# Attention and feed-forward over 16 batches on one core: x2T in two PSUM banks, the blocks' sum in two halves, three moved pieces of work

## What is computed

```
x = x + xattn(layernorm(x), ctx, ctx)
  scores = einsum(qg, kg) * scale            # per pair of blocks, 64 x 64
  attn = softmax(scores)                     # over the block's 64 keys
  out = segment_sum(attn @ vg, rows) @ Wo.T
x = x + ffn(layernorm(x))
  shared  = relu(xf @ sw1 + sb1) @ sw2 + sb2          # hidden size 1024
  routing = expert top1(token): relu(xf @ w1[e] + b1[e]) @ w2[e] + b2[e]
```

## Time and profile before

| | us |
|---|---|
| runs (median of 3) | 946.83 (944.99 to 947.7) |
| the profiled execution's own time | 948.77 |
| its span in the profile | 946.6 |
| PE busy | 807.7 (85%) |
| DVE busy | 598.4 (63%) |
| ACT busy | 493.3 (52%) |
| POOL busy | 420.3 (44%) |

### The profile page before, as it was taken

How to read it: one execution, slowest core, us unless ns; L and a number is a source line. 1 busy time by engine, 2 the same in 40 slices (tenths; PEclk the granted TensorE clock), 3 DMA queues, 4 the chain that set the end, 5 groups by cost and what they waited for, 6 DMA issues and landing times.

```text
span 946.6 us, 23198 instructions
## 1 busy us (share of the span) xinstructions
PE 807.7 (85%) x7862; PEld 670.6 (71%) x7862; DVE 598.4 (63%) x1226; ACT 493.3 (52%) x1108; POOL 420.3 (44%) x773
## 2 busy tenths in 40 slices
PE   3277877899998999898999989898989899988984
PEld 3146656586877868685968778686869596868884
DVE  3767584676758575776767575757577676646331
ACT  2373444436465555546464646455564646465542
POOL 3644324334344453635445544445363554455401
PEclk8587998979999999999999999999999999999998
DMA  8657232244435244344454453534434444414720
GB/s 269 172 150 252 78 102 67 76 137 142 151 110 185 88 147 149 107 148 136 135 153 144 128 172 95 172 110 133 152 115 137 152 133 137 142 46 134 253 83 23
DMA packets 97386, 128.17 MB, mean 135 GB/s; under 512 B 14655, under 2 KB 82623, under 8 KB 97088
## 3 DMA queue, kind: packets, MB, share of 16 engines
q1 hardware_dynamic: 89760, 107.89, 37.3%
q0 software_dynamic: 6624, 18.95, 5.9%
q10 hardware_dynamic: 960, 0.79, 0.4%
HBM read 90.80 MB, written 37.04 MB: 135 GB/s over the span
## 4 chain that ended last, share of the span: by engine, by line
PE 58%; DVE 15%; DMA 12%; ACT 6%; SPq 3%; issue 3%; POOL 1%; ACTq 1%; POOLq 0%; DVEq 0%
PE hid L502 19%; PE acc L671 13%; PE nd L596 10%; DVE T L1144 5%; DMA QP<-scratch_m 5%; PE work L580 4%; DMA scratch_m<-mT 3%; PE work L624 3%; PE work L502 2%; PE work L555 2%; DVE nmax L1125 2%; PE work L610 2%; DVE T L1141 2%; ACT h L925 1%; DVE Xs L1078 1%
## 5 line engine op out<-in xcount | busy, mean ns | idle before, releaser
L1404 POOL TENSOR_TENSOR hl<-h,hh 128x256 fp32r<-128x256 f32 x228 | 169.0, 744 | 351.2 <-ACT hh L925 351.1
L908 ACT ACTIVATE PT<-work 128x512 f32<-128x512 f32 x256 | 139.3, 600 | 58.4 <-PE work L580 55.8
L1144 DVE RECIPROCAL T<-nd 128x256 f32<-128x256 f32 x64 | 112.1, 1752 | 77.8 <-PE nd L596 74.0
L925 ACT ACTIVATE h<-hid,bias 128x256 f32<-128x256 f32 x144 | 69.0, 480 | 117.1 <-PE hid L502 117.1
L502 PE MATMUL hid<-Xs,W 128*128 128x256 f32 x816 | 115.1, 296 | 10.8 <-DVE Xs L1078 10.8
L502 PEld LDWEIGHTS hid<-Xs,W 128*128 128x128 f32 x816 | 105.1, 199 | 17.7 <-issue 10.8
L671 PE MATMUL acc<-w_hi,hh 128*128 128x256 f32 (+1 forms) x528 | 110.7, 292 | 0.0
L671 PE MATMUL acc<-w_lo,hh 128*128 128x256 f32 (+1 forms) x528 | 105.4, 281 | 0.0
L502 PE MATMUL hid<-Xr,W 128*128 128x256 f32 x768 | 105.3, 287 | 0.0
L596 PE MATMUL nd<-PT,V 128*32 128x256 f32 x1024 | 83.3, 398 | 25.4 <-DVE T L1146 22.5
L1125 DVE TENSOR_REDUCE nmax<-work 128x8 f32<-128x512 f32 x128 | 82.3, 685 | 35.1 <-PE work L555 35.0
(11 more groups left out here) (184 smaller groups left out, 1511.5 us busy)
## 6 DMA issues: line engine op xcount, KB each, us to landing
W<-w1q SPq DMA_DIRECT2D x64, 512.0 KB, 5.6
KP<-scratch_k SPq DMA_DIRECT2D x192, 64.0 KB, 2.3
QP<-scratch_q SPq DMA_DIRECT2D x180, 64.0 KB
scratch_k<-T SPq DMA_DIRECT2D x16, 512.0 KB, 3.5
scratch_q<-T SPq DMA_DIRECT2D x16, 512.0 KB, 3.3
yt<-yq SPq DMA_DIRECT2D x17, 260.0 KB, 2.8
xt<-xq SPq DMA_DIRECT2D x17, 256.0 KB, 3.8
xin<-x SPq DMA_DIRECT2D x16, 256.0 KB, 3.8
```

What stands on the lines that cost most here:

```text
L908: nc.scalar.activation(PT[:, j % 4].rearrange("p t q -> p (t q)"), work[:, BANK[("st", j)], :], ACT.Exp).then_inc(sem["exp_done"], 1)
L925: last = nc.scalar.activation(dst, hid[:, u % 2, a, :], ACT.Relu, bias=bias[:, 2 * u + a:2 * u + a + 1])
L1144: nc.vector.reciprocal(T[:, p, :], nd[:, p % 2, 1, :]).then_inc(sem["inverted"], 1)
L1404: nc.gpsimd.tensor_tensor(R(hl[:, u % 2, a]), h32[:, u % 2, a], hh[:, u % 2, a], ALU.subtract).then_inc(sem["hl_done"], 1)
```

## The change

Seven edits, all in the order of work or in where it is put:

1. `prep_tokens` puts the first chunk of x2T in the first half of its `work` bank and the second chunk in `hid[:, 1, 0]`; each chunk has its own high and low part on ACT and DVE (128x256 each in place of 128x512), and `shared_up(n, 0)` waits for the second chunk only halfway through its first product.
2. `attention_out` runs in two halves: the first waits for pairs 0 to 3 of T, the second for all eight. 32 matmuls of 64 columns in place of 16 of 2x64.
3. On PE each `shared_down` stands one place later: 0 behind visit 2, 1 behind visit 3, 2 behind the tile's transposes, 3 behind the q projection. ACT's `shared_relu(n, 3)` moves behind the split of mT, DVE's `finish_shared` behind q's low part.
4. The guessed pairs of iterations 3 to 15 are 2, 5, 7 in place of 2, 3, 6, 7.
5. Batch 1's x and context are loaded ahead of batch 0's bounces through DRAM, and its norm stands ahead of batch 0's maxima on DVE (before, in their middle); POOL's part of it stands ahead of the weights' splits.
6. ACT splits the first four weight pieces ahead of issuing its 12 spreads of q, not behind.
7. Behind the loop, the last batch's tile transposes stand behind `shared_up(3)` and `shared_down(2)`, and SP loads two registers ahead of the weights, not behind.

```diff
-GUESSED_EARLY, GUESSED = (1, 3, 5, 7), (2, 3, 6, 7)
+GUESSED_EARLY, GUESSED = (1, 3, 5, 7), (2, 5, 7)
-    "x2T": ("x2_lo", 1), "xr": ("xr_lo", 1), "rk": ("ranked", 1),
+    "x2T": ("x2_lo", DC), "xr": ("xr_lo", 1), "rk": ("ranked", 1),
+        def x2T_chunk(c):
+
+            return work[:, BANK["x2T", 0], 0:SEQ] if c == 0 else hid[:, 1, 0, :]
...
                 for n, (s, m) in enumerate(steps):
+                    if second and n == len(steps) // 2:
+                        pe.wait_ge(*second)
...
-                pe.wait_ge(sem["t_done"], PAIRS * (i + 1))
-                pairs = T[:, :, :].rearrange("p (c q) t -> p q c t", c=DC)
-                for r in range(NBLK):
-                    queries = slice(BLOCK * r, BLOCK * r + BLOCK)
-                    for q in range(4):
-                        mm = nc.tensor.matmul(bank[32 * q:32 * q + 32, :, queries], hsum[:, r, :],
-                                              pairs[:, q, :, queries], start=True, stop=True)
+                for c in range(DC):
+                    pe.wait_ge(sem["t_done"], PAIRS * i + 4 * c + 4)
+                    for r in range(NBLK):
+                        queries = slice(BLOCK * r, BLOCK * r + BLOCK)
+                        for q in range(4):
+                            mm = nc.tensor.matmul(bank[32 * q:32 * q + 32, c, queries], hsum[:, r, :],
+                                                  T[:, 4 * c + q, queries], start=True, stop=True)
...
                 pe.wait_ge(sem["ln2_done"], i + 1)
-                transposes(bank, xhat2, "x2T_full")
+                if type(i) is not int or i > 0:
+                    pe.wait_ge(sem["relu_done"], 2 * last_odd(i) + 2)
+                transposes(bank, xhat2, "x2T_full", apart=hid[:, 1, 0, :])
...
-                    shared_down(n, 0)
                 visit(i, 2, more)
                 if shared:
+                    shared_down(n, 0)
                     shared_up(n, 2)
+                visit(i, 3, more)
+                if shared:
                     shared_down(n, 1)
-                visit(i, 3, more)
...
```

More of the change, by code:

```diff
@@ L250, in guess_count @@
         def guess_count(i, p):
-            return len(GUESSED) * i + guessed(i).index(p) + 1
+            done = guessed(i).index(p) + 1
+            if type(i) is int and i < 3:
+                return len(GUESSED_EARLY) * i + done
+            return len(GUESSED) * i + 3 * (len(GUESSED_EARLY) - len(GUESSED)) + done
         def inverses(i, p):
-            return (PAIRS - len(GUESSED)) * i + p + 1 - sum(q <= p for q in guessed(i))
+            done = p + 1 - sum(q <= p for q in guessed(i))
+            if type(i) is int and i < 3:
+                return (PAIRS - len(GUESSED_EARLY)) * i + done
+            return (PAIRS - len(GUESSED)) * i + done - 3 * (len(GUESSED_EARLY) - len(GUESSED))
         def shared_unit(n, u):
@@ L460, in _ @@
                     .then_inc(sem["padded"], 16)
+            rows = [sp.value_load(left[0:1, e:e + 1], min_val=0, max_val=QROWS - TILE) for e in range(2)]
             for u in range(UNITS):
@@ L501, in split_product, with transposes @@
                 for n, (s, m) in enumerate(steps):
+                    if second and n == len(steps) // 2:
+                        pe.wait_ge(*second)
                     mm = nc.tensor.matmul(dst, R(s), R(m), start=n == 0, stop=n == len(steps) - 1)
                 return mm
-            def transposes(bank, src, done):
+            def transposes(bank, src, done, apart=None):
                 for c in range(DC):
                     for t in range(TT):
-                        mm = nc.tensor.transpose(bank[:, SEQ * c + P * t:SEQ * c + P * t + P],
-                                                 src[:, t, P * c:P * c + P], id32[:, :])
-                mm.then_inc(sem[done], 1)
+                        to = bank[:, SEQ * c + P * t:SEQ * c + P * t + P]
+                        if apart is not None and c > 0:
+                            to = apart[:, P * t:P * t + P]
+                        mm = nc.tensor.transpose(to, src[:, t, P * c:P * c + P], id32[:, :])
+                    if apart is not None or c == DC - 1:
+                        mm.then_inc(sem[done], 1)
             def front_xT(n, bank=None):
@@ L646, in ranks, with up @@
                                  skip_group_check=True).then_inc(sem["rk_full"], 1)
-            def up(g, u, weights, tokens):
+            def up(g, u, weights, tokens, second=None):
                 if type(g) is not int or g >= 2:
@@ L654, in up @@
                                        [(weights[:, u, 0, c, cols], weights[:, u, 1, c, cols]) for c in range(DC)],
-                                       [(tokens[:, 0, c, :], tokens[:, 1, c, :]) for c in range(DC)])
+                                       [(tokens[:, 0, c, :], tokens[:, 1, c, :]) for c in range(DC)],
+                                       second if a == 0 else None)
                 mm.then_inc(sem["hid_full"], 1)
@@ L767, in iteration @@
                 if tile:
+                    shared_down(n, 3)
                     tile_up(m, 0)
@@ L842, in _ @@
             shared_down(last, 1)
-            tile_tokens(last, work[:, 0, :])
             shared_up(last, 3)
             shared_down(last, 2)
+            tile_tokens(last, work[:, 0, :])
+            shared_down(last, 3)
             tile_up(last, 0)
-            shared_down(last, 3)
             tile_up(last, 1)
@@ L940, in tokens_high @@
             def tokens_high(i):
-                high(i, "x2T_full", work_bank("x2T"), Xs[:, 0], "x2_hi")
+                for c in range(DC):
+                    high(DC * i + c, "x2T_full", x2T_chunk(c), Xs[:, 0, c], "x2_hi")
             def table_relu(e):
@@ L967, in iteration @@
                     splits(i, u + 1)
-                    if tile or shared and u < UNITS - 1:
+                    if shared and u < UNITS - 1:
                         shared_relu(n, u)
@@ L1037, in _ @@
             projection_high(3)
+            for n in range(EARLY_PIECES):
+                split_high(n)
             act.wait_ge(sem["first_q_bounced"], 16)
@@ L1043, in _ @@
             front_v(0, acc[:, :, :])
-            for n in range(EARLY_PIECES):
-                split_high(n)
             iteration(0, False, False, True)
@@ L1056, in _ @@
             tile_relu(last - 1, 3)
-            for u in range(UNITS - 1):
+            for u in range(UNITS):
                 shared_relu(last, u)
             tile_high(last, work[:, 0, :].rearrange("p (c t) -> p c t", c=2))
-            shared_relu(last, UNITS - 1)
             tile_relu(last, 0)
@@ L1191, in shared_low @@
             def shared_low(i):
-                low(i, "x2_hi", work_bank("x2T"), Xs[:, 0], Xs[:, 1], "x2_lo")
+                for c in range(DC):
+                    low(DC * i + c, "x2_hi", x2T_chunk(c), Xs[:, 0, c], Xs[:, 1, c], "x2_lo")
             def tile_low(n, src, tokens=Xr):
@@ L1341, in _ @@
                     split_low(n)
+            norm1_apply(1)
             for j in range(4):
```

39 lines of the change are left out of this document (21 added, 18 removed).

## The result

The changed kernel takes 935.5 us (median of 5 runs, 933.55 to 941.65), the kernel before 944.99 (5 runs in the same series, 943.21 to 947.7). The ratio is 0.990, 95% interval 0.987 to 0.993: 9.5 us faster, a measured gain of 1%. The forecast was 930.0 with a range of 919 to 942. The profiled execution of the changed kernel is the slowest of its five (941.65, of which 939.5 are the span); the one of before took 948.77. So the two profiles differ by 7.1 only, and where the time went is read from stretches that are alike, not from the ends.

A forecast was written before the change was run, and what follows sets the result against it. PE's matmuls and the short waits between them were taken as the bound. Terms -7.2 (loop), -6, -1.3, -2.8, -1.9, -1.0 and +1.7 (clock) sum to -18.5 from 948.77; it took 930, range 919 to 942.

The forecast's parts named there:

- One sign that the prediction had named for being wrong: In the profile after: a clock of 0.5 to 0.8 in many iterations would show the forecast wrong.
- 0.7 for x2T: Loop iteration, PE's wait before the first shared_up: two banks gain 0.7 us, at least 0.3, at most 0.76.
- pairs and halves: Loop iteration's second part: new guessed pairs and attention_out in halves end it 1.2 us earlier (0.4 to 1.7).
- The rival in which halves cost as much as the whole: attention_out: each half costs 1.0 us, 0.35 less gained in each of 12 iterations, 934; chance 0.1.
- The late downs: Loop iteration, visit 2: shared_down one place later gives PE a new wait of 1.6 us for DVE's maxima (1.2 to 1.9).
- the first part: Loop iteration from x2T to the first values: ends 0.6 us later (0 to 1.2), ACT's relus and exps bounding its end.
- one more fall: Granted clock in the loop: the new waits at visit 2 lower it once more, +1.7 us (0 to +7).
- slower, by a fall in each iteration: Loop: the new wait lowers the clock in each iteration, 1.7 us for each of 13, 950; chance 0.06.
- The start: DVE's chain to batch 0's last maxima: stats, wait for rstd and xhat go out of it, -6 us (-3 to -8).
- the rival in which the start gains little, because the spreads are late: Start: spreads late in the full DMA queues, so little is gained there, 934; chance 0.1.
- Batch 0's end, iterations 1 and 2: Half sum and split x2T win 1.3 us at batch 0's end; earlier visits win 2.8 in iterations 1 and 2.
- Iteration 15 and behind the loop: Iteration 15: -1.9 us, its new wait being shorter; behind the loop, shorter waits for tokens and a transfer: -1.0.

The follow-up runs named there:

- e1: The changed kernel with all shared_down and their relu and sum put back to their old places, the rest of the change kept: 918.7 us.
- e8: e1 with the guessed pairs 2, 3, 6, 7 again in place of 2, 5, 7: 929.36 us.
- e7: e1 with attention_out in one piece again, behind all eight pairs: 920.25 us.
- e3: The changed kernel with shared_down(0) alone put back ahead of the second visit: 922.85 us.
- e5: The changed kernel with x2T's two chunks in one bank again, split in one pass on each engine: 936.3 us.
- e2: The kernel before with only the shared_down, their relu and sum moved one place later: 956.85 us.
- e10: e1 with the loads of x and context of batch 1 placed behind the two bounces: 919.16 us.
- e12: e1 with the edits of e9 and e10 together: 917.96 us.
- e6: e1 with the start undone: batch 1's loads, norm and deviation and ACT's early splits in their old places: 920.74 us.
- e4: The changed kernel with its edits behind the loop undone: 936.03 us.
- e11: e1 with the edits behind the loop undone: 917.44 us.
- e9: e1 with the bias issued ahead of three weight units and the next tile's tokens ahead of W1's last two units: 919.54 us.

## Why the prediction was right, and where it was off

**Sign, size, mechanism.** Faster was right, and 935.5 lies in the forecast's own 923 to 936, at its upper end. It is 5.5 above the point forecast. The gain is 9.5 where 16.8 were forecast; 1.8 of what is missing comes of the kernel before, which ran at 945.0 here and not at 946.8. Profile against profile the forecast was further off: -7.1 for -18.5, as the profiled execution of the changed kernel is 6.1 above its median. So that the median lies inside the range owes something to luck. By the stretches above, the clock, the start and the part behind the loop are what was put too well, and a period without a fall gained more than forecast. One sign that the prediction had named for being wrong came in part: a clock near 0.57 in five iterations of 12.

**x2T, pairs, halves.** Predicted 0.7 for x2T. In the old order (e1) all three together give 51.5 - 49.55 = 1.95, of which pairs are 0.8 and halves 0.4 (e8, e7), and 0.75 is left for x2T, which was not undone alone in that order. Predicted for pairs and halves was 1.2; measured 0.8 + 0.4. These steps hold within 0.1. The second half costs 0.58, where I took 0.65 with 0.5 as the lower bound. The rival in which halves cost as much as the whole is out.

That half is 32 instructions of 64 columns in 0.58 us, 18 ns each. The Trainium skill, TensorE: Matmul & The Clock Gate, section Back-to-back issue gap, gives an issue floor of some 25 ns for each, and by that page it would be 0.8 us, an estimate. The trace does not agree: it has 0.58, with four column groups in turn.

**The late downs.** I had put this move at a cost of 1.3 an iteration (the first part 0.6 later in spite of x2T's 0.7), and an iteration at 50.8. Measured 1.1 (e1 against the changed kernel) and 50.65; 0.85 gained where I had 0.6 to 0.65. So the prediction knew that one part of the change ate more than half of what the others give, and the wait at visit 2 stands where it was forecast: 0.54 and 0.69 for 0.7 and 0.9. The wait of 0.41 to 0.47 for the shifted rows was not worth removing in this way: it is back in e1, which is the faster kernel. One step was wrong in its reason: I said that the end of the first part is then set by ACT's relus and exps. There is a wait for ACT, but only of 0.35; e3 shows that the waits at visit 2 are most of the 1.1.

**The clock: the mis-sized term.** I had one more fall, +1.7. There were four more in the 12 periods, and what they took is 5 x 1.6 less the 0.6 of before, 7.4; with 12 x 0.85 = 10.2 gained, that makes the -2.8 of the table. e1, e3 and e5 take the waits away or shorten the first, and the falls are gone. I had argued that two waits of 1.6 together, behind the pairs, lowered the clock once in 12, and that new ones of the same size would do so once. That was wrong, and the sum of the waits alone does not decide it. Behind the pairs, 0.47 and 1.13, 2.2 us apart, gave one fall in 12 in the kernel before and in e2, and two in e8. At visit 2, 0.54 and 0.69, 1.2 us apart, gave five, though their sum is smaller; 0.2 and 0.69 gave none in e2 and none in e5. The rival "slower, by a fall in each iteration" had the mechanism and its price right; with five of 12 it took back most of what the iterations won, and not the sign.

The Trainium skill, TensorE: Matmul & The Clock Gate, section A second HAM failure mode: psum-queue depth-cycling, describes a kernel whose PE pauses briefly and often around its PSUM banks and whose clock goes back and forth between the two levels; the rows of this kernel agree, with waits of 0.5 and 0.7 us for banks that DVE still reads and a granted clock of 0.57 behind them.

**The start.** Predicted -6, and the two profiles differ by 4.1 at the first maxima. DVE's stats, norm and wait went out of its chain as forecast: PE's wait for the last maxima is 2.19, where it was 6.98. PE's timeline shows what came in their place (the earlier trace rows is the last of them before):

```profile
28.48 0.79 PE L570 MATMUL work<-KP,QP 48*128 48x256 f32 x4 [10.70 <-DMA QP<-scratch_q]
34.10 0.79 PE L570 MATMUL work<-KP,QP 48*128 48x256 f32 x4 [4.40 <-DMA QP<-scratch_q]
...
43.42 0.47 PE L585 MATMUL work<-id,nmax 128*128 128x128 f32 x1 [2.19 <-DVE nmax L1154]
```

The first score came 1.9 later, and the second visit waits 4.40 for its spread, where it waited 3.01 for DVE before. I had let the delay of the spreads and the gain of ACT's early splits cancel; the delay won. That is the rival in which the start gains little, because the spreads are late; that full queues are the reason is not shown, since e10 and e12 issued the spreads earlier and the first score came no sooner. e6 against e1 leaves 0 to 2 us for the whole start in time, so -6 was too much by 4 or more.

**Batch 0's end, iterations 1 and 2.** Predicted -4.1, the profiles say -5.0; the waits before batch 1's and 2's transposed maxima fell from 2.43 each to 0.85 and 0.69, 3.3 together for the 2.8 forecast. The waits were right; what they are worth is not shown. e1 has the old order and both waits of 2.43 again, and its stretch is 157.2, shorter than the changed kernel's 159.9.

**Iteration 15 and behind the loop.** Predicted -2.9, the profiles say +4.8. For the edits behind the loop the times say nothing that can be told: e4 is 0.5 above the changed kernel and e11 1.3 below e1. What I missed is in SP's queue: with the order moved, the relus of the tile come to wait for a bias that had been early enough before, as it stands behind three weight units. I had looked at PE's waits and named relu, low part and sum as the next bound, but not the 4 KB in front of the relu.

## What to carry to other kernels

Work that is moved out of one wait leaves the place where it stood: ask first what it was covering there. Here one `shared_down` hid the DVE maxima of the visit ahead. Moving it cost 0.7 us of the 1.1 that the late order costs in an iteration, and the falls of the clock. Judge each part of a change in the order in which it will stand: the split of x2T is worth 0.75 a period in one order, and in the other 0.35 less what it does to the clock. Issuing one transfer ahead of others can move the wait to the next: in e9 PE's waits behind the loop went from 4.09 and 0.70 to 1.54 and 3.54, and the time stayed.

## What the runs showed of the hardware

The granted clock fell to its lower level behind two PE waits of 0.42 to 0.55 and 0.69 us, 1.2 us apart from start to start, in 5 of 12 iterations (the changed kernel and e4), and in none of 12 when the first wait was 0.2 (e2 and e5). Behind two waits of 0.47 and 1.13, 2.2 us apart, it fell once or twice in 12 (before, e2, e8). A fall cost 1.6 us where PE was busy throughout, and 0.6 to 0.8 in these three, where a wait of PE followed it. 32 instructions of fp32 matmuls with 64 columns in four column groups took 0.58 us to the next start, with 128 columns 1.01.
